# Bidirectional GRU over 1024 time steps: the candidate scan's result in SBUF in place of a PSUM bank

## What is computed

```
def step(h, xt):
    gh = h @ whh.T + bhh
    xr, xz, xn = jnp.split(xt, 3, axis=-1)
    hr, hz, hn = jnp.split(gh, 3, axis=-1)
    r = jax.nn.sigmoid(xr + hr)
    z = jax.nn.sigmoid(xz + hz)
    n = jnp.tanh(xn + r * hn)
    h_new = (1.0 - z) * n + z * h
    return (h_new, h_new)
...
yf = _gru_dir(z @ gru_wih_f.T + gru_bih_f, gru_whh_f, gru_bhh_f, False)
yb = _gru_dir(z @ gru_wih_b.T + gru_bih_b, gru_whh_b, gru_bhh_b, True)
y = jnp.concatenate([yf, yb], axis=-1) @ out_w.T + out_b
return x + y.reshape(Bx, Hx, Wx, C)
```

## Time and profile before

| | |
|---|---|
| median of 3 runs | 1733.62 us (1731.27 to 1734.33) |
| the profiled execution | 1740.94 us, its span 1739.1 us |
| TensorE busy | 1622.2 us (93%) |
| VectorE busy | 1496.9 us (86%) |
| ScalarE busy | 1191.5 us (69%) |
| DMA | mean 18 GB/s |

### The profile page before, as it was taken

One profiled execution on the slowest core, in us unless ns is written; L12 is line 12 of the kernel. 1 busy time (PEld: TensorE's weight loads), 2 busy tenths in 40 slices (PEclk: granted clock), 3 DMA queues, 4 the chain that ended last, 5 costly groups with the idle time before them and its releaser, 6 DMA issues.

```text
span 1739.1 us, 61541 instructions
## 1 busy us (share of the span) xinstructions
PE 1622.2 (93%) x21570; PEld 1287.0 (74%) x21570; DVE 1496.9 (86%) x9055; ACT 1191.5 (69%) x6271; POOL 57.1 (3%) x126
## 2 busy tenths in 40 slices
PE   3547999999999999999999999999999999999997
PEld 2435777777777777777777777777777777777776
DVE  7879888888888888888888888888888888888887
ACT  6735667777677776767667777677767677677766
POOL 5520000000000000000000000000000000000000
PEclk9755555555555555555555555555555555555555
DMA  5200000000000000000000000000000000000000
GB/s 159 80 7 8 12 14 11 15 11 14 12 14 12 12 13 11 14 12 15 11 14 7 13 13 13 11 14 11 15 11 15 11 14 12 13 13 13 13 13 16
DMA packets 40102, 31.04 MB, mean 18 GB/s; under 512 B 3448, under 2 KB 37624, under 8 KB 39800
## 3 DMA queue, kind: packets, MB, share of 16 engines
q1 hardware_dynamic: 39800, 27.13, 5.4%
HBM read 18.73 MB, written 8.39 MB: 16 GB/s over the span
## 4 chain that ended last, share of the span: by engine, by line
DVE 69%; ACT 21%; issue 8%; PE 1%; DMA 0%; POOL 0%; SPq 0%; DVEq 0%; ACTq 0%; POOLq 0%
DVE state L895 30%; ACT drive L498 21%; DVE bank L884 18%; DVE halves L904 12%; DVE big L876 4%; DVE seq L860 1%; DVE stats L732 1%; DVE weighted L758 1%; DMA gamma_row<-in_gamma 0%; DVE moments L737 0%; PE bank L541 0%; PE bank L545 0%; PE bank L594 0%; POOL xin L363 0%; PE bank L528 0%
## 5 line engine op out<-in xcount | busy, mean ns | idle before, releaser
L594 PEld LDWEIGHTS bank<-halves,wsplit 128*128 128x128 f16 x18432 | 726.9, 107 | 348.3 <-DVE halves L904 257.9
L594 PE MATMUL bank<-halves,wsplit 128*128 128x16 f16 x18432 | 901.7, 182 | 47.6 <-DVE halves L904 44.6
L895 DVE TENSOR_TENSOR_SCAN state<-gain,drive 128x48 f32<-128x48 f32 x2048 | 526.9, 257 | 175.3
L594 PE MATMUL bank<-seq,wcomb 128*128 128x128 f32 x1536 | 592.9, 482 | 0.2 <-DVE seq L860 0.2
L492 ACT ACTIVATE rpair<-bank 128x16 f32<-128x16 f32 x2048 | 379.4, 185 | 246.3 <-PE bank L594 246.3
L498 ACT ACTIVATE drive<-bank 128x16 f32<-128x16 f32 x2048 | 395.2, 193 | 220.5 <-DVE bank L884 16.4
L884 DVE TENSOR_TENSOR_SCAN bank<-rpair,bank 128x32 f32<-128x32 f32 x2048 | 459.3, 224 | 3.4 <-ACT rpair L492 3.4
L904 DVE SCALAR_TENSOR_TENSOR halves<-state 128x32 f16<-128x32 f32 x2048 | 398.7, 195 | 35.5
L495 ACT ACTIVATE gain<-bank 128x16 f32<-128x16 f32 x2048 | 393.0, 192 | 31.6
L594 PEld LDWEIGHTS bank<-seq,wcomb 128*128 128x128 f32 x1536 | 385.9, 312 | 0.7 <-DVE seq L860 0.7
L911 DVE SCALAR_TENSOR_TENSOR drive<-gain,state 128x16 f32<-128x16 f32 x2046 | 365.6, 179 | 0.0
(11 more groups left out here) (115 smaller groups left out, 203.1 us busy)
## 6 DMA issues: line engine op xcount, KB each, us to landing
xin<-in_x SPq DMA_DIRECT2D x16, 512.0 KB, 3.5
big<-in_x SPq DMA_DIRECT2D x124, 64.0 KB
out<-big SPq DMA_DIRECT2D x124, 64.0 KB
wih<-in_wiht SPq DMA_DIRECT2D x2, 384.0 KB
con<-in_consts SPq DMA_DIRECT2D x1, 424.0 KB, 5.0
whh<-in_whht SPq DMA_DIRECT2D x2, 192.0 KB
xin<-in_x SPq DMA_DIRECT2D x4, 64.0 KB
out<-xin SPq DMA_DIRECT2D x4, 64.0 KB
```

What stands on the lines that cost most here:

```text
L594: return nc.tensor.matmul(o, w, m, start=start, stop=True, skip_group_check=True)
L895: v.tensor_tensor_scan(state[:, d, ring, :], gain[:, e, cols], drive[:, e, cols], 0.0, ALU.mult, ALU.subtract).then_inc(state_ready[d], 1)
```

## The change

`cand` becomes an SBUF tensor of 128 columns instead of the eighth PSUM bank. No instruction is added, removed or moved: the candidate scan (line 884) writes its 32 columns to SBUF, and the tanh (line 498) reads its 16 from there. The eighth bank is still used in the first stage through `bank[7]`. Both `rpair` and NX stay where they are.

```diff
     gain = sb("gain", [P, 2, 3 * COLS])
+    cand = sb("cand", [P, 4 * COLS])
...
     R, Z, NX, Y = bank[0:2], bank[2:4], bank[4:6], bank[6]
-    cand = bank[7]
```

## The result

The changed kernel takes 1746.76 us (median of 4 runs, 1745.99 to 1747.69), the kernel before 1733.15 (4 runs, 1731.27 to 1734.33). The ratio is 1.0071, with a 95% interval of 1.0051 to 1.0090: 0.7% slower, some 13 us. I had forecast 1764.3, +30.7 us. TensorE's granted clock was 0.50, the level of 1.2 GHz, from 120 to 1720 us in both profiled executions, so the clock is no part of the difference.

The account below looks back on a forecast made before the run. The prediction took one direction's loop, with one scan and one tanh, to bound the step at 1.57 us. Tanh +32 and scan -2 gave +30 ns over 1024 steps, 30.7 us: 1733.6 to 1764.3 us, range 1749 to 1788.

Parts of the forecast that it names:

- The tanh, +32 ns: ScalarE's tanh reading SBUF in place of PSUM goes from 193 to 225 ns, once per step in a direction's loop.
- The scan, -2 ns: VectorE's candidate scan writing SBUF in place of PSUM goes from 228 to 226 ns, once per step in a direction's loop.
- The one-direction loop is what sets the 1.57.: Direction 0's loop from scan through tanh, state, halves and reset sigmoid to the next scan binds, at 1.57 us a step.
- TensorE is not short of throughput: On TensorE, 257.9 us of weight loads idle for halves were taken to show that its queue does not bind.
- VectorE's loop takes it twice: VectorE's order, with two scans and two tanhs, grows from 1.52 to 1.58 us, under 1.60, so it doesn't bind.
- Both tanhs count: Rival: VectorE's order binds with two tanhs a step, 0.06 us more a step, 1795 us; chance 0.05.
- They cancel, or the tanh's extra time is covered: Rival: TensorE's queue releases the reset sigmoid, or a 196 ns scan offsets the tanh; no change, 1734 us; chance 0.03.
- The write to PSUM was the dear part: Rival: the scan's PSUM write hides latency, so an SBUF scan under 196 ns makes it faster, 1717 at 180; chance 0.09.

Follow-up runs that it names:

- scan only: Kernel before, with the scan writing SBUF while the tanh still reads the PSUM bank's old values: 1725.3 us, ratio 0.9932.
- tanh only: Kernel before, with the scan still writing PSUM while the tanh reads a constant SBUF tile: 1762.51 us, ratio 1.0150.
- direction 0 in SBUF: Kernel before, with cand in SBUF for direction 0 alone, nothing left out: 1738.57 us, ratio 1.0013.
- direction 1 in SBUF: Kernel before, with cand in SBUF for direction 1 alone, nothing left out: 1739.64 us, ratio 1.0013.
- Z first, PSUM: Kernel before, with direction 1's matmuls on TensorE in the order R, Z, N in place of R, N, Z: 1717.82 us, ratio 0.9901.
- Z first, SBUF: Changed kernel, with direction 1's matmuls on TensorE in the order R, Z, N: 1748.62 us, ratio 1.0073 to the kernel before.
- the shorter projection: Input projections stream 16 columns in place of 128: on the kernel before 1722.5 us, ratio 0.9919; on the changed kernel 1746.13 us, ratio 1.0067.

## Why the prediction came out as it did

Three loops hold all the runs (ns a step, summed from the distances above, with the scans' unheld durations in VectorE's order). The column of one direction has 343 ns from the end of halves to the reset sigmoid, that is without any wait for TensorE. The longest loop of a row should be the measured step.

| | one-direction loop | TensorE's queue | VectorE's order | measured |
|---|---|---|---|---|
| before | 1540 | **1562** | 1528 | 1564 |
| scan only | 1532 | **1555** | 1512 | 1554 |
| tanh only | 1572 | 1562 | **1592** | 1592 |
| direction 0 in SBUF | **1565** | 1555 | 1552 | 1567 |
| direction 1 in SBUF | **1565** | 1562 | 1552 | 1570 |
| after | 1565 | 1555 | **1576** | 1576 |
| Z first, PSUM | **1540** | cut | 1528 | 1545 |
| Z first, SBUF | 1565 | cut | **1576** | 1576 |

The two rows that are 5 ns off are those in which direction 1's own loop binds; its matmuls wait a few ns for the bias fillings ahead of them (345 and 348 ns in place of 343). The third loop was read from the traces, and no expectation gave its length in advance; the runs with the scan alone, with the shorter projection and with the new order bear it out.

*The tanh, +32 ns.* Right: 225 ns measured. The pair of one-column activations carried over to sixteen columns. The Trainium skill's "Perfetto Trace Analysis", section Optimizing Scalar/DVE Operations, has 93 - 51 = 42 ns of busy time between ScalarE's two sources; these runs show 32. The Trainium skill's "ScalarE: Activation LUTs", section What ACT_TABLE_LOAD costs, would as an estimate have made it 207 in all with the strided output; the trace shows 225.

*The scan, -2 ns.* Mis-sized: -8. The 228 that I held it against had 7 ns of waiting in it, which the all-SBUF estimate of 226 did not show. By 32 - 8 in place of 32 - 2 the sum would have been 24.6 us, 1758: inside the range. The Trainium skill's 65 ns between VectorE's two memories, from the same section of "Perfetto Trace Analysis", are not to be seen when the output moves.

*"The one-direction loop is what sets the 1.57."* **This is the step that failed.** The prediction took the 0.37 us from halves 0 to the reset sigmoid for a fixed part of direction 0's loop, on the ground that *"TensorE is not short of throughput: its weight loads stood idle 257.9 us waiting for halves"*. The idle time is real, but the timeline has it in front of direction 1's matmuls (0.20 at 1002.01), none in front of direction 0's at 1001.35. These found TensorE still at the projection, which had itself been held up by the N matmuls' wait for scan 0. So 21 of the 365 ns were a wait, direction 0's loop was 1540 ns long and not 1564, and the 1564 were set by the loop through TensorE's queue, which holds no tanh. The net +25 ns of tanh and scan first used up the slack of direction 0's loop: 1540 + 25 = 1565, one ns over what the step had been, in place of +30.

*"VectorE's loop takes it twice: 1.52 + 0.06 = 1.58, still under 1.57 + 0.03 = 1.60, so it doesn't bind."* The 1.58 was right (1576 ns), in part by luck. The waits in this order were 11 ns in front of scan 0, and 7 and 18 inside the scans, where the prediction had 30 and 20; this gives 1528 for its 1520. The change added 64 - 16 = 48 for its 60. The 1.60 that it was held against was not right, since it rested on the step above. VectorE's order takes over at 1576, and the step goes from 1564 to 1576: +12 ns, 1024 x 12 = 12 us.

So where did the missing 18 us go? They fell into the slack under the third loop: with that loop cut the kernel before takes 1545 ns a step and not 1564, and from there to 1576 it is the whole 31. The check on this is the new TensorE order, which cuts it. With it in place beforehand, the very same edit costs 1748.62 - 1717.82 = 30.8 us, a step of 1576 in place of 1545. I had forecast 30.7, but that they agree is chance: there it is VectorE's order with two tanhs against a loop with one.

*The rivals.* "Both tanhs count" is what happened to the mechanism, with a far smaller price than its 61 us, because VectorE's order started 36 ns below the step and the scans gave 16 back. "They cancel, or the tanh's extra time is covered" had 0.03, and it named TensorE's queue, the right one. I argued it away by a total of idle time. "The write to PSUM was the dear part" is out: 8 ns.

**The better version** is the kernel before with direction 1's matmuls in the order R, Z, N: 1717.8 us, 1.0% faster than before and 1.7% faster than the changed kernel, with nothing left out.

## What to carry to other kernels

In a hand-ordered recurrence, write down every closed loop through a step (one direction, each engine's order, and loops that pass from one direction to the other through a queue), with its own length and with what it holds. A cost on a loop that is not the longest is free up to that loop's slack, and a cost counts only from where its loop becomes the longest. An engine's total idle time does not show that it is free where the path crosses it: look at what it was doing when that work arrived, instruction by instruction. When a tile moves to another memory, price its writer and its reader apart: here the tanh pays 32 ns for the read from SBUF, and the scan gains 8 on the write.

## What the runs showed of the hardware

A VectorE instruction's recorded duration may hold a wait. In the kernel before, scan 1 was recorded at 229, 224, 214 and 202 ns where it started 31, 36, 47 and 62 ns after the end of its reset sigmoid, so that it ended 260 to 264 ns after that. In the run of the tanh's half alone, where it started 69 ns or more after the sigmoid's end, its duration stood at 203 ns (201 to 206). The same scan is 18 ns longer behind the elementwise instruction than behind the scan: 221 and 203 with the result in PSUM, 213 and 195 in SBUF. And ScalarE's tanh of 16 columns took 223 to 229 ns from SBUF, in all 2048 instructions, where it took 192 to 198 from PSUM. Between the end of scan 0 and the first weight load of the N matmuls that wait for it lay 52 to 55 ns in every step from 30 to 999 of the kernels before and after and of the four experiments with one half of the change.
